# A filter matrix with seven moment columns behind each part, and a first transfer of two channels

## The reference

```python
res = conv3x3(x, W_id, b_id)
cA, cH, cV, cD = _swt2_level3(x[0])
...
low_att = _attention(cA_t, DCT_LOW, W_dl, b_dl, W_al, b_al, W1_low, W2_low)
high_att = _attention(high, DCT_HIGH, W_dh, b_dh, W_ah, b_ah, W1_high, W2_high)
dmt = jnp.concatenate([low_att, high_att], axis=1)
out = jax.nn.leaky_relu(conv3x3(dmt, W_enc, b_enc), 0.01)
return out + res
...
x = x + _L0_conv_ref(_gn(x), ...)
```

## Time and profile before

| | |
|---|---|
| median of 3 runs | 1970.77 us (1967.54 to 1971.35) |
| the profiled execution | 1965.66 us, of which its span is 1963.7 us |
| TensorE busy | 1934.4 us (99%) |
| VectorE, ScalarE, GpSimd busy | 1464.4, 1008.3, 1032.8 us |
| start of the first matmul | 8.31 us |
| end of `before_maps` on TensorE | about 183 us |

### The profile page before, as it was taken

The page is one execution under the profiler, slowest core; times in us unless marked ns, Lnnn a source line. Parts: engine busy times, 40 slices in busy tenths (PEclk is TensorE's granted clock), DMA queues, the critical chain, the costliest instruction groups (busy, mean ns, idle before and its releaser), DMA issues.

```text
span 1963.7 us, 79515 instructions
## 1 busy us (share of the span) xinstructions
PE 1934.4 (99%) x35530; PEld 1609.5 (82%) x35530; DVE 1464.4 (75%) x2253; ACT 1008.3 (51%) x1067; POOL 1032.8 (53%) x775
## 2 busy tenths in 40 slices
PE   8999999999999999999999999999999999999998
PEld 7987999999999999668897888767877778766664
DVE  5665578778878876577777777777777777777776
ACT  4555666666666676634444344434444444444432
POOL 0005878887888885444444444444444444444444
PEclk9999999999999999999999999999999999999999
DMA  8883598888888884588888877887887878877774
GB/s 172 238 289 98 166 276 214 218 214 216 209 219 215 209 215 104 134 202 205 198 205 208 199 204 197 207 200 194 201 210 198 200 202 206 204 201 199 206 207 124
DMA packets 132647, 391.92 MB, mean 200 GB/s; under 512 B 49676, under 2 KB 50448, under 8 KB 118128
## 3 DMA queue, kind: packets, MB, share of 16 engines
q1 hardware_dynamic: 132336, 387.10, 77.2%
HBM read 258.56 MB, written 128.45 MB: 197 GB/s over the span
## 4 chain that ended last, share of the span: by engine, by line
PE 36%; issue 33%; POOL 26%; ACT 1%; DVE 1%; DMA 1%; POOLq 1%; SPq 0%; DVEq 0%; ACTq 0%
POOL stage L1689 26%; PE ps L1097 13%; PE ps L1063 7%; PE ps L621 5%; PE ps L1067 5%; PE ps L1066 3%; PE ps L623 3%; POOLq L1687 1%; DMA big<-in_x 1%; DVE pool_of L1284 0%; DVE pool_of L1272 0%; DMA pool_of<-in_x 0%; POOL pool_of L1358 0%; POOL pool_of L315 0%; POOL pool_of L306 0%
## 5 line engine op out<-in xcount | busy, mean ns | idle before, releaser
L1689 POOL TENSOR_TENSOR stage<-stage,big 128x448 f32<-128x448 f32 x448 | 511.5, 1142 | 642.7 <-DVE stage L1664 639.9
L1601 PE MATMUL ps<-pool_of,w_hi 64*64 64x448 f16 x12096 | 645.9, 350 | 3.7 <-issue 3.3
L1601 PEld LDWEIGHTS ps<-pool_of,w_hi 64*64 64x64 f16 x12096 | 450.4, 107 | 147.3 <-issue 8.7
L1601 PE MATMUL ps<-pool_of,w_lo 64*64 64x448 f16 x8064 | 452.4, 350 | 2.2 <-issue 2.2
L1601 PEld LDWEIGHTS ps<-pool_of,w_lo 64*64 64x64 f16 x8064 | 304.5, 107 | 98.3 <-issue 4.8
L1664 DVE SCALAR_TENSOR_TENSOR stage<-ps,w_max,pool_of 64x448 f32<-64x448 f32 x448 | 305.9, 683 | 45.7 <-PE ps L1601 33.0
L1284 DVE BATCH_NORM_STATS2 pool_of<-big 128x6 f32<-128x448 f32 x392 | 232.5, 617 | 76.8 <-DMA big<-in_x 76.6
L1515 ACT ACTIVATE pool_of<-pool_of 128x2240 f16<-128x2240 f32 x56 | 126.4, 2258 | 313.9 <-PE ps L1601 313.9
L1664 DVE SCALAR_TENSOR_TENSOR stage<-ps,w_max,xs 64x448 f32<-64x448 f32 x384 | 262.1, 683 | 33.5 <-PE ps L1601 22.1
L1515 ACT ACTIVATE pool_of<-xs,pool_of 128x2240 f16<-128x2240 f32 x48 | 108.4, 2258 | 284.4 <-PE ps L1601 284.4
L1601 PE MATMUL ps<-big,w_hi 64*64 64x448 f16 x4032 | 225.4, 350 | 0.0
(11 more groups left out here) (197 smaller groups left out, 2487.4 us busy)
## 6 DMA issues: line engine op xcount, KB each, us to landing
out<-stage SPq DMA_DIRECT2D x448, 224.0 KB, 3.2
big<-in_x SPq DMA_DIRECT2D x392, 224.0 KB, 5.2
pool_of<-in_x SPq DMA_DIRECT2D x104, 560.0 KB, 7.0
xs<-in_x SPq DMA_DIRECT2D x96, 560.0 KB, 7.1
pool_of<-row_filtered SPq DMA_DIRECT2D x110, 224.0 KB, 3.8
pool_of<-in_x SPq DMA_DIRECT2D x32, 392.0 KB, 7.4
row_filtered<-big SPq DMA_DIRECT2D x2, 6272.0 KB, 22.7
row_filtered<-big SPq DMA_DIRECT2D x4, 1568.0 KB, 8.9
```

The lines of the kernel that those rows point to most:

```text
L1601: mm = pe.matmul(psum[4 * p + 2 * g + r][C * k:C * k + C, 0:NT], w[lanes, t, :], v[lanes, y:y + 2, kx:kx + W], start=(j == 0), stop=(j == ...
L1689: pool.tensor_tensor(stage[p][:, r, g, :], stage[p][:, r, g, :], e_map[:, e:e + NT], ALU.add)\
```

## The change

- The 14 sum columns no longer stand together behind the two parts: seven stand behind the 112 low columns and seven behind the 112 high columns, each filter's own. `last_rows` now cuts out the last 56 columns of both parts in an even pass; in an odd pass it is 49, as before. ScalarE's and VectorE's copies read two pieces of 112, and two of 7, that lie 119 columns apart in PSUM, in place of 224 and 14 in one piece.
- The first group's two transfers become four: channels 0 and 1 of both halves with a semaphore of their own (`pair_in`), then channels 2 to 7. TensorE waits for `pair_in` ahead of channel 0 and for `group_in[0]` ahead of channel 2; VectorE waits for both before it measures.
- TensorE waits for `ones_set`, then multiplies `ones` by itself 16 times into bank 7, ahead of its wait for `fh_in`. The results are not used.

```diff
-    fh = np.concatenate([low.T[:, :HR], high.T[:, :HR], moved, low.T[:, HR:], high.T[:, HR:]], axis=1)
+    fh = np.concatenate([low.T[:, :HR], moved[:, :NF], high.T[:, :HR], moved[:, NF:], low.T[:, HR:], high.T[:, HR:]], axis=1)
...
+        pair_in = sem(top, "pair_in")
...
-                for hc in range(2):
-                    src = x[0, g * CG:g * CG + CG, hc * HALF:hc * HALF + HALF, wc * HALF:wc * HALF + HALF]
-                    sp.dma_start(xg[g][:, hc, :, :], src.rearrange("c h w -> h c w")).then_inc(group_in[g], 16)
+                for a, b, signal in ((0, 2, pair_in), (2, CG, group_in[0])) if k == 0 else ((0, CG, group_in[g]),):
+                    for hc in range(2):
+                        src = x[0, g * CG + a:g * CG + b, hc * HALF:hc * HALF + HALF, wc * HALF:wc * HALF + HALF]
+                        sp.dma_start(xg[g][:, hc, a:b, :], src.rearrange("c h w -> h c w")).then_inc(signal, 16)
...
-            def last_rows(v, base, reach):
+            def last_rows(v, base, length):
 
-                return v[:, base + KEPT - HR + reach:base + KEPT + HR + reach].rearrange("p (s r) -> p s r", s=2)[:, :, HR - reach:HR]
+                return v[:, base:base + 2 * length].rearrange("p (s r) -> p s r", s=2)[:, :, KEPT:length]
 
+            pe.wait_ge(ones_set, 1)
+            for k in range(16):
+                pe.matmul(small[:, 0:P], ones[:, :], ones[:, :], start=True, stop=True)
             pe.wait_ge(fh_in, 16)
...
-                reach = HR + NG - KEPT if hh == 0 else HR - KEPT
+                length = HR + NF if hh == 0 else HR
                 for c in range(C):
                     n, g = C * k + c, c // CG
-                    if hh == 0 and c % CG == 0:
+                    if n == 0:
+                        pe.wait_ge(pair_in, 32)
+                    elif n == 2 or hh == 0 and c % CG == 0:
                         pe.wait_ge(group_in[g], 32 * wc + 32)
...
-                        ps = psum[bank][0:HALF, 0:256]
-                        ins = act.copy(rows[hh][:, :, :, c].rearrange("w r s -> w s r"),
-                                       ps[:, 0:2 * HR].rearrange("w (s r) -> w s r", s=2))
+                        length = HR + NF if hh == 0 else HR
+                        ps = psum[bank][0:HALF, 0:2 * length].rearrange("w (s r) -> w s r", s=2)
+                        ins = act.copy(rows[hh][:, :, :, c].rearrange("w r s -> w s r"), ps[:, :, 0:HR])
                         if hh == 0:
-                            ins = act.copy(u_sum[:, wc, :, c], ps[:, 2 * HR:N0])
+                            ins = act.copy(u_sum[:, wc, :, c].rearrange("w (s u) -> w s u", s=2), ps[:, :, HR:length])
...
                     dve.wait_ge(group_in[g], 32 * wc + 32)
+                    if k == 0:
+                        dve.wait_ge(pair_in, 32)
```

More of the change, by code:

```diff
@@ L621, in tensor @@
                     pe.matmul(o[:, 0:width], xg[g][:, near, c % CG, :], fh[:, near, first:first + width], start=True, stop=False)
-                    far_out = last_rows(psum[bank][0:HALF, :], 0, reach)
-                    pe.matmul(far_out, xg[g][:, far, c % CG, :], last_rows(fh[:, far, :], first, reach),
+                    far_out = last_rows(psum[bank][0:HALF, :], 0, length)
+                    pe.matmul(far_out, xg[g][:, far, c % CG, :], last_rows(fh[:, far, :], first, length),
                               start=False, stop=True).then_inc(product, 1)
@@ L856, in vector @@
                         dve.wait_ge(product, n + 1)
-                        ps = psum[bank][0:HALF, 0:256]
-                        ins = dve.tensor_copy(rows[hh][:, :, :, c].rearrange("w r s -> w s r"),
-                                              ps[:, 0:2 * HR].rearrange("w (s r) -> w s r", s=2))
+                        length = HR + NF if hh == 0 else HR
+                        ps = psum[bank][0:HALF, 0:2 * length].rearrange("w (s r) -> w s r", s=2)
+                        ins = dve.tensor_copy(rows[hh][:, :, :, c].rearrange("w r s -> w s r"), ps[:, :, 0:HR])
                         if hh == 0:
-                            ins = dve.tensor_copy(u_sum[:, wc, :, c], ps[:, 2 * HR:N0])
+                            ins = dve.tensor_copy(u_sum[:, wc, :, c].rearrange("w (s u) -> w s u", s=2), ps[:, :, HR:length])
                         ins.then_inc(dve_rows, 1)
```

## The result

The changed kernel took 1958.96 us in the median of 6 runs (1957.16 to 1961.37), the kernel before 1969.83 us in the median of its 6 (1965.66 to 1971.91). The ratio is 0.9947, with a 95% interval of 0.9934 to 0.9961: some 10.4 us less, where 5.3 were forecast. Two later comparisons with 12 runs of the changed kernel each gave 0.9967 (0.9958 to 0.9977) and 0.9969 (0.9953 to 0.9984), 6 to 7 us. Single runs of the same program differ by up to 16 us (1961.69 to 1977.73 in one repeat of the kernel before).

What follows compares the result with a forecast made beforehand. TensorE, busy 99% of the span, was taken as the bound. Fewer columns (2.3 us) and an earlier start (3.0) sum to 5.3 us: 1960.4 against the profiled 1965.66, 1965.4 against the median; range 1960.3 to 1968.6.

Steps and rivals of the forecast that it cites:

- the lower end of the range: Whole kernel: 1960.3 us, set 5.3 us below the profiled execution, the fastest seen.
- Term 1, the far matmul: Passes 0 and 2: 112 columns in place of 126 make a channel 598.2 ns, 18.5 ns less; 2.3 us in all.
- Term 2, the start: Start of pass 0: two channels loaded earlier and the clock raised by ones bring channel 4 forward by 3.0 us.
- The rest of group 0 lands at 8.2 to 8.3: First loads: channels 2 to 7 land then, behind the pair, as the group's bytes are the same in all.
- Channel 2 beyond 9: Sign of a wrong forecast: channel 2 of pass 0 starting after 9 us, where 8.4 was expected.
- if the clock rises 3.5 us after the first one: TensorE's ones at the start: full clock from 4.7 us, ones end at 6.4, channel 0 starts about then.
- The split of the 3.0 us: Start: 2.4 us from the first two channels not following the group's landing, 0.6 from the clock in channels 2 and 3.
- Small transfers: Rival, chance 0.10: the pair's small transfers occupy the queue longer, the start gains 0.1 us, time 1968.4 us.
- From there on the chain holds no time that does not move with TensorE: From pass 3 on: no other wait was expected to change the gain of 5.3 us.
- The copies: Rival, chance 0.05: ScalarE's copies of two pieces take 1.19 us a pair and become the bound; 1984 us.
- wait in pass 2 at channel 11: Rival, chance 0.10: VectorE's late transfer keeps its time, TensorE stands there and gain is lost; 1966.7 to 1969.6 us.
- The first: Rival, chance 0.13: all 16 ones run at the lower clock and hold TensorE until 8.0 us; 1966.3 to 1968.2 us.

Runs made afterwards that it cites:

- pair_only: The kernel before with only channels 0 and 1 of the first group in transfers and waits of their own; ratio 1.0005 (0.9995 to 1.0015) to the kernel before.
- after_h48: The changed kernel with 48 multiplications of one column added behind the excite stage of pass 3; ratio 0.9993 (0.9980 to 1.0005) to the kernel before.

## Why the prediction was wrong

The measured time of 1958.96 us fell below the range, whose lower end was 1960.3. The direction and the two mechanisms held, and the sum of 5.3 us lies within what 12 runs show for the changed kernel (interval 4.5 to 8.3 us, and 3.2 to 9.3). That it does is in part luck: the start gave less than forecast, and the block borders, which the sum did not have, made up for it. Two steps failed: that nothing behind the first stage moves except with TensorE, and the lower end of the range.

- **Term 1, the far matmul: right.** Forecast 598.2 ns a channel, measured 598.4, and 2.3 us; the floor of the odd pass's far matmul was the right row to take. Its two instructions take 98.3 ns each at 112 columns as at 98. That the floor is the next weights' load stays a reading; no run changed the weights.
- **Term 2, the start: right in kind, 3.0 us forecast, 1.8 measured** (4.08 less 2.3; in the two repeats of the changed kernel pass 3 starts 5.55 and 4.78 us earlier, which leaves 3.2 and 2.5). Two steps were off. "The rest of group 0 lands at 8.2 to 8.3" was 9.11 here (8.07 and 8.79 in the repeats), and group 1 was late at 13.13, because the loads ran slower in this execution. "Channel 2 beyond 9" stood among the signs of being wrong. These are the windows of 8 to 13 us, of the changed kernel and of the repeat of before, whose last column is the rate:

```profile
8.00:13.00 5.00, 4.50 (x29) 3.82 (x27) 2.98 (x11) 2.29 (x9) 0.00 (x0) 1.00 1.19 207
```
```profile
8.00:13.00 5.00, 5.00 (x21) 4.38 (x22) 1.72 (x7) 1.13 (x4) 0.00 (x0) 1.00 1.19 258
```

  The second was "if the clock rises 3.5 us after the first one": it rose at 6.40 us, 5.3 us after, so channel 0 started at 7.3 and not at 6.4. That cost nothing, as forecast for such a delay. The split of the 3.0 us, 2.4 by the first two channels and 0.6 by the clock, does not stand: the ones alone gave 1.96 us at pass 3, the pair alone 0.98, and the pair beside the ones 0.57.
- **Small transfers: not slow.** The pair's first transfer landed 3.4 us after its issue, at 4.6, the second 0.4 us behind it, as by their bytes, and channel 0 of `pair_only` started at 5.12, where I had 5.8. The Trainium skill, DMA: Bandwidth & Descriptors, section Bandwidth, says "descriptor-dominated" only of transfers under 64 KB, and those of the pair have 98 KB.
- **"From there on the chain holds no time that does not move with TensorE": this step failed.** It is true of waits between engines, and I looked for no other. The kernel before already had stops of TensorE without a releaser, 6.6 us in its trace, which stand where instruction blocks begin. The change adds 64 instructions and moves them all. That they move is shown; that this is worth about 1.5 us is the account over the groups above.
- **The range and the scatter.** With 4.7 us from the first stage (three traces of the changed kernel against two of before) and 1.5 from the borders, 6.2 us are accounted for, which is what both comparisons with 12 runs show. The 10.4 us of the first comparison had six runs on each side, and neither of the larger ones repeats it. What the 4 us between them are stays open. My lower end was the forecast taken from the fastest execution of before, as if that could not be undercut: the repeats of before alone spread from 1961.69 to 1977.73.
- **The rivals.** None occurred as written. The copies kept 548 and 544 ns; TensorE has no wait in pass 2 at channel 11. The first came near: in `after_h48`, whose start is that of the changed kernel, 30 of the 32 passes of the ones were slow, and channel 0 started at 7.84.

## What to carry to other kernels

A matmul with few columns has a floor: read it from the narrowest matmul already in the trace before counting columns. Ahead of a first matmul that waits for data, use the wait to raise the clock (2 us here); to bring two channels' data earlier was worth 0.6 to 1 us. And when TensorE's program is written out at length, any change in its number of instructions moves its block borders and with them the stops, which are 4 to 14 us in all here: a gain of a few microseconds has to be confirmed with the instruction count held or padded, and with a dozen runs or more.

## What the runs showed of the hardware

- The clock rose at very different times after the same work. From the first multiplication of ones at 1.12 us, passes of 213 ns turned into passes of 112 ns at 4.6, 5.1, 5.1, 6.4, 6.6, 6.6, 7.0, 7.3 and 7.6 us in nine executions. In the last of these, 30 of the 32 passes were slow.
- The rate of the first loads varied from 207 to 273 GB/s between executions of the same kind. With the pair it was 207 to 258 (ten traces), without 235 to 273 (eight), so the split may cost some of it; no run here separates that from the execution's own rate.
- TensorE's stops for instructions stand at block borders, 187 of 187, and not at every border: of the 278 or 279 blocks of an execution 5 to 20 cost 0.3 us or more.
- The same stop of TensorE of about 2 us was followed by about ten groups of matmuls at the 1.2 GHz level in three traces (before, `pair_only`, `after_h48`) and by none in four others. That alone is about 1.7 us of the scatter (4 us at a mean granted clock of 0.57).
